# Latent attention: the products with the values of each half row in one burst of 32 in place of two of 16

## The reference, cut to what matters

```
kv_c = rms_norm(x @ W_kv) * g_kv ;  q_c = x @ W_q
k = concat(heads(kv_c @ W_kdec, 8), rope(heads(x @ W_krope, 32)))
q = concat(heads(q_c @ W_qdec, 8), rope(heads(q_c @ W_qrope, 32)))
v = heads(kv_c @ W_vdec, 8)
scores = (q @ k^T) / sqrt(40), -inf above the diagonal
out = (softmax(scores) @ v) @ W_o
```

## Time and profile before

| what | value |
|---|---|
| median of three runs | 2362.21 us |
| the profiled execution | 2350.24 us, its span 2348.4 us |
| TensorE busy over the span | 1970.9 us (84%) |
| VectorE, ScalarE, GpSimd busy | 1403.9, 1173.3, 729.9 us |
| products with the values (L1948), busy | 1024 MATMULs, 47.8 us |

### The profile page before, as it was taken

One profiled execution on the slowest core, in us unless ns is written; L12 is line 12 of the kernel. 1 busy time (PEld: TensorE's weight loads), 2 busy tenths in 40 slices (PEclk: granted clock), 3 DMA queues, 4 the chain that ended last, 5 costly groups with the idle time before them and its releaser, 6 DMA issues. The chain is left out here.

```text
span 2348.4 us, 68942 instructions
## 1 busy us (share of the span) xinstructions
PE 1970.9 (84%) x28845; PEld 1250.0 (53%) x28845; DVE 1403.9 (60%) x2804; ACT 1173.3 (50%) x1869; POOL 729.9 (31%) x759
## 2 busy tenths in 40 slices
PE   5577899996959999787699989458998957999997
PEld 1232577763326777532555559325555414667765
DVE  5544788753568887255577735547775054556562
ACT  5663466654526666464366644325666441333333
POOL 0202666741057666201233103522220013222220
PEclk8787899998979999898699989759999987899999
DMA  3000000000000000000545520223441012433441
GB/s 136 0 0 1 2 3 3 3 3 1 0 1 3 3 3 3 2 0 5 160 121 128 137 60 28 77 57 95 98 99 43 0 41 91 133 124 119 139 127 39
DMA packets 93704, 122.43 MB, mean 52 GB/s; under 512 B 9376, under 2 KB 80384, under 8 KB 90048
## 3 DMA queue, kind: packets, MB, share of 16 engines
q1 hardware_dynamic: 91352, 113.84, 17.3%
q0 software_dynamic: 2048, 4.20, 0.6%
HBM read 67.62 MB, written 49.15 MB: 50 GB/s over the span
## 5 line engine op out<-in xcount | busy, mean ns | idle before, releaser
L1671 ACT ACTIVATE at_pr<-ps 128x768 f32<-128x768 f32 x256 | 203.9, 811 | 92.4 <-PE ps L1572 86.9
L1060 POOL TENSOR_TENSOR la_tc<-la_ta,la_tb 128x512 f32<-128x512 f32 x128 | 162.7, 1271 | 112.2 <-DVE la_tb L1356 108.2
L1077 PE MATMUL ps<-w_l0f,la_hs 128*128 128x512 f32 x256 | 152.7, 681 | 47.0 <-DVE la_tb L1356 40.7
L1996 ACT ACTIVATE at_pr<-ps 128x640 f32<-128x640 f32 x128 | 90.0, 703 | 179.4 <-PE ps L1899 179.4
L2038 DVE TENSOR_REDUCE at_m<-ps 128x2 f32<-128x512 f32 (+3 forms) x256 | 113.4, 485 | 105.7 <-PE ps L1899 102.1
L1716 DVE TENSOR_REDUCE at_m<-ps 128x2 f32<-128x512 f32 x256 | 174.2, 680 | 0.0
L2289 POOL TENSOR_TENSOR at_parts<-at_ta,at_tb 128x512 f32<-128x512 f32 x64 | 81.2, 1269 | 246.7 <-DVE at_tb L2279 242.7
L1047 POOL TENSOR_TENSOR la_qn<-la_tc,la_rn 128x512 f32<-128x512 f32 x128 | 133.9, 1046 | 52.9 <-issue 36.9
L1715 DVE TENSOR_REDUCE at_m<-ps 128x2 f32<-128x256 f32 x256 | 107.7, 421 | 67.2 <-PE ps L1572 62.7
L1572 PE MATMUL ps<-cast 64*64 64x256 bf16 x2048 | 146.3, 276 | 0.0
L1354 DVE TENSOR_TENSOR la_ta<-ps,la_tab 128x512 f32<-128x512 f32 x128 | 88.2, 689 | 95.7 <-ACT la_sq L1280 95.7
(11 more groups left out here) (380 smaller groups left out, 4872.9 us busy)
## 6 DMA issues: line engine op xcount, KB each, us to landing
scratch_latent<-at_parts SPq DMA_DIRECT2D x32, 640.0 KB
at_qs<-scratch_latent SPq DMA_DIRECT2D x32, 320.0 KB
at_ks<-scratch_latent SPq DMA_DIRECT2D x32, 320.0 KB
scratch_alibi<-at_parts SPq DMA_DIRECT2D x32, 192.0 KB
at_ks<-scratch_alibi SPq DMA_DIRECT2D x32, 192.0 KB
scratch_rope<-at_parts SPq DMA_DIRECT2D x32, 192.0 KB
at_ks<-scratch_rope SPq DMA_DIRECT2D x32, 192.0 KB
w_l0f<-in_l0f SPq DMA_DIRECT2D x2, 1689.5 KB, 15.6
```

The costliest lines, as they stand in the source:

```text
L1060: nc.gpsimd.tensor_tensor(tc[:, x, :], ta[:, x % 2, :], tb[:, x % 2, :], ALU.add).then_inc(s.la_tc, 1)
L1077: nc.tensor.matmul(ps[:, 0, :], hs[:, i % QSLOTS, t * P:(t + 1) * P], w("wq" if p < 2 else "wk"), start=True, stop=True).then_inc(s.la_pro ...
L1671: nc.scalar.activation(pr[:, p % RING, :, :], ps[:, at:at + 2, 0:384], ACT.Exp, scale=scale).then_inc(s.at_prob, 1)
```

## The change

The table that says in which turns `values` is called, and for which half and blocks, is cut from four calls to two: all four blocks of the first half at x = 1, and all four of the second half at x = 5. The semaphore goes up by four a call and not by two, so that it still reaches eight a row.

```diff
-        VALUES = {0: (0, (0, 1)), 1: (0, (2, 3)), 4: (1, (0, 1)), 5: (1, (2, 3))}
+        VALUES = {1: (0, (0, 1, 2, 3)), 5: (1, (0, 1, 2, 3))}
...
-                m.then_inc(s.at_attended, 2)
+                m.then_inc(s.at_attended, 4)
```

## The result

The first comparison gave 2371.97 us against 2359.98 us, medians of ten runs each, ratio 1.0051 (1.0030 to 1.0071). Two repetitions gave 1.0015 (0.9991 to 1.0039) and 1.0035 (1.0016 to 1.0055). Their mean, weighted by the intervals, is 1.0035 (1.0023 to 1.0048), or +8.4 us (5.5 to 11.3); the forecast was +7.1 us. Within one comparison, single executions of either kernel lie 14 to 32 us apart from lowest to highest, and the kernel before against itself gave 1.0014 (0.9990 to 1.0038), so the traces decide more here than the times.

What follows compares the result with a forecast made beforehand. TensorE, busy 21.61 of 22 us a steady row, was taken as the bound. Steps 5 to 15 (5.4), 4 (0.95), 16 (0.29), 17 (-0.2), 18 (0.69) and 19 (-0.05) gave +7.1: 2362.2 to 2369.3 us, range 2362.8 to 2374.9.

Steps and rivals of the forecast that it cites:

- Part 1: At x = 0, without its burst, TensorE stalls 0.43 us for VectorE's maxima; scores of x = 1 come 0.46 us earlier.
- Part 2: At x = 1, the burst of 32 takes 1.22 us, not 1.36 as two bursts; each merge saves 0.14 us.
- rival B: Merging bursts saves nothing in steady rows, which take 1.36 us; +11.3 us in all, 2373.5 us; chance 0.10.
- Part 3: At x = 4 and 5, a stall of 0.33 us and a burst longer by 0.75; net +0.20 us a row.
- Step 4: Scores already wait for the maxima, so the removed burst gives nothing back: 0.75 at x = 1 plus 0.20, +0.95 us.
- Steps 18 and 19: The last steps, without scores: +0.69 us in the first of them and -0.05 us in the second.
- Rival A: TensorE-bound alone, maxima not late: 30 merges of 0.14 won, nothing lost; -4.2 us, 2358.0 us; chance 0.08.
- Rival C: TensorE's unexplained gaps in steps 6 and 15 vanish during the new stalls; +5.4 us, 2367.6 us; chance 0.10.
- A fall of the granted clock I rule out.: Over the steady rows: clock stays 1.00, as at 2318 to 2332 with 2.6 us idle of 14; 1.1 of 22 to come.
- the wait for the loaded row: In step 17 of the changed trace, TensorE's wait for the loaded row was to be about 0.96 us.
- the 12 us: Profiled execution before stood 12 us below the median, for reasons put outside this stage as far as the trace tells.

Runs made afterwards that it cites:

- e3: Kernel before with only the first half's bursts joined, at x = 1; the second half stays at x = 4 and 5; ratio to before 1.0008.
- e4: Kernel before with only the second half's bursts joined, at x = 5; the first half stays at x = 0 and 1; ratio to before 1.0000.
- e6: Changed kernel with part of VectorE's cosine and sine products at x = 3 and 7 left out in rows after the first; ratio to before 0.9980.
- e2: Kernel before with both halves in bursts of 32, but at x = 0 and x = 4; ratio to before 0.9986.
- e12: Kernel before, unedited, compared against itself, with a second trace on another chip; ratio 1.0014.
- e11: Kernel before, with the last row's load sent only after the scores of turn 4 of step 16; ratio to before 1.0004.
- e10: Changed kernel, with the last row's load bringing only the first half of the columns; ratio to before 1.0004.
- e7: Kernel before with bursts of 32 at x = 0 and x = 4, the one of x = 0 ahead of turn_back; ratio to before 0.9962.
- e1: Changed kernel again, unedited; ratio to before 1.0015, medians 2365.13 and 2359.82 us.
- e9: Changed kernel a third time, unedited; ratio to before 1.0035, mean 8.5 us above before.

## Why the prediction was right, and what in it was not

- *Part 1, the lost cover at x = 0*: right. Scores 0.80 us behind turn_back, as worked out. The idle time in the trace is 0.36, not the 0.43 announced, because the sum went from start to start, and the trace counts from the last modelled end, 0.07 later; the same holds for 0.26 in place of 0.33 at x = 5. e3, e4 and e6 show the cause.
- *Part 2, a merge saves 0.14 us*: right in every row at full clock, and not only behind a wait (1.22 or 1.23 us in steps 4 to 19 of the changed trace, but 1.54 in step 17, where the clock had fallen); rival B falls. The Trainium skill's rule (page "TensorEngine Tiling (Array Packing)", Key Properties) that a change of tiling mode drains TensorE agrees with it. No run here tells a drain from another cost of entering a burst. e2's period of 21.70 shows the gain without the loss.
- *Part 3*: right, +0.20 a row (e4).
- *Step 4, which pays its whole burst*: +0.96 measured, 0.95 forecast. It was read from one row, in which TensorE waited already with the cover. *Steps 18 and 19*: +0.68 and -0.04, forecast 0.69 and -0.05.
- *Rival A* needs VectorE early by 0.43 us. In e6 VectorE is early by 0.34 of it, and the change turns into a gain, so the mechanism and its deciding point were right and the rival's condition was absent.
- *Rival C* came in part. The two gaps were 2.9 us together in the first trace before, but 0.95 in e12; in the changed kernel's three they were 0.8, 0.5 and 0.7. The gap of step 6 comes and goes in both kernels. That of step 15 was 1.77, 0.95 and 1.49 us in the three traces with the order before (e11 the third) and 0.10, 0.18, 0.74 and 0.09 in the four with the changed order (e10 the fourth), so some 1.1 us of the forecast's 7.1 may be won back there. That the stalls do it is not shown: e7, which has none, has 0.44.
- *What failed: "A fall of the granted clock I rule out."* It rested on a stretch in which idle time came in pieces under 1 us. The same stretch tells nothing of a longer wait in one piece. The clock did fall in step 17 of all three traces of the changed kernel, and in none of two before. The step named for it, the wait for the loaded row, was put at 0.96 us and came as 1.36, 1.55 and 2.03; before it was 0.82 and 1.32. Over thirteen traces the clock fell right behind this wait where it was 1.36, 1.41, 1.55, 1.71, 2.03 or 2.35 us, and not where it was 0.24, 0.78, 0.82, 0.87, 0.96, 1.09 or 1.32. That the wait brings the fall is supported by e10 and e11; that this makes up the difference between 7.1 and 8.4 us is not shown, as both lie in the interval. The forecast came right with this term at nothing and without the gain at step 15, two omissions that work against each other.
- *Two readings of the trace before*. The page's clock is 7 and 8 in the first two of its last seven slices, not near full. The stage's early steps lie there, at half clock, and their length moves the time by as much as the change does. And the 12 us by which the profiled execution stood below the median were put outside this stage: from the first scores to the end the first trace has 377.4 us, e12, the same kernel on another chip, 385.0, and the early steps of e11 are 6.8 us longer than the first trace's too, so some of them lay in this stage.
- *Open*: why the last load lands later in the changed kernel beyond the 0.14 us that the shorter turns 4 to 7 explain. Sorted afterwards, the unhindered traces fall in two groups: the wait was 1.36, 1.41, 1.55, 1.71 and 2.03 us in the five that join the second half at x = 5 (changed, e6, e1, e4, e9), and 0.24 to 1.32 in the seven that don't. From the load's issue to the scores were 9.32 to 10.01 us in the first group and 8.35 to 9.43 in the second. No run was made to test this.

## What to carry to other kernels

Where one engine is full and another is late only at certain places, it matters in which turn the full one does its independent work. Before joining bursts, look for the end of the late engine's chain in each turn and put the joined burst there, not behind it: the same join changed the period by -0.27 us in the covering turns (e2) and by +0.49 behind them. Join in the covering turn, and ahead of the instruction that waits (e7).

## What the hardware showed that I had not expected

A late start of full clock in the stage's first steps moved the time by as much as the change: 6.9 us between two traces of the same kernel, before and e12. Behind a single wait near the stage's end the clock fell. In e9 the 10 us around and behind that wait had 122 matrix products, where 216 stood in the kernel before. By the estimate above such a fall cost 1.7 to 4.9 us, behind waits of 1.36 to 2.35 us and not in the order of their lengths, while the three waits of 0.26 to 0.36 us in every steady row left the clock at 1.00. Such a wait can so cost more than its own length; that it is dearer in sum than the 23 short ones is not shown.
